# Double-buffering the hidden tile of the scan stage, moving the carry table into its loop, and squaring with an accumulator

## What is computed

```python
x = L0_attn_x
x = x + _L0_attn_ref(_layernorm(x), W, lam_logit, eta, gamma, beta)
#   z = x @ W.T ; m_t = lam[k] * m_(t-1) + z_t  for 4 decays k
#   h = z + sum_k eta[k] * m[..., k] ; layer norm of h, * gamma + beta
x = x + _L0_ffn_ref(_layernorm(x), SU_ug, SU_dp, ...)
#   fwht(x * SU_ug)/64 -> W_up, W_gate -> silu(gate) * up
#   -> fwht(. * SU_dp)/64 -> W_down
```

## Time and profile before

| what | value |
|---|---|
| time, median of 2 runs | 6996.12 us (6816.88 and 7175.36) |
| profiled execution, its own time | 6800.32 us |
| its span on the slowest core (core 7) | 6798.7 us |
| spans of the 8 cores | 6772.5 to 6798.7 us |
| busy: PE, DVE, ACT | 51%, 35%, 14% of the span |
| tables end, first prefix chunk starts | 62.4 us |
| scan stage, its first `pz` to its last store | 1067.3 to 2025.6 us |
| up/gate stage starts | 2463.0 us |

### The profile page before, as it was taken

How to read it: one execution, slowest core, us unless ns; L and a number is a source line. 1 busy time by engine, 2 the same in 40 slices (tenths; PEclk the granted TensorE clock), 3 DMA queues, 4 the chain that set the end, 5 groups by cost and what they waited for, 6 DMA issues and landing times.

```text
span 6798.7 us, 50228 instructions; the slowest of 8 cores (6772.5 to 6798.7 us)
## 1 busy us (share of the span) xinstructions
PE 3484.6 (51%) x16543; PEld 1515.4 (22%) x16543; DVE 2380.4 (35%) x2879; ACT 956.1 (14%) x2027; POOL 220.8 (3%) x423
## 2 busy tenths in 40 slices
PE   0111114222661179999999999211121494756652
PEld 0000001000220024444444444000000142322321
DVE  5565562111446611111111111355434532332322
ACT  3444440000112230000000000211121000000000
POOL 0000001000000000000000000000000110000100
PEclk9999997656765579999999999555555797888876
DMA  4445449999111111111111111211321563645453
GB/s 76 85 84 85 85 69 121 126 124 124 58 68 44 54 33 59 57 56 56 56 56 56 60 60 53 61 50 50 81 68 50 145 181 92 179 107 162 125 155 67
DMA packets 413911, 574.26 MB, mean 84 GB/s; under 512 B 34201, under 2 KB 329693, under 8 KB 403421
## 3 DMA queue, kind: packets, MB, share of 16 engines
q1 hardware_dynamic: 355710, 403.25, 19.3%
q0 software_dynamic: 57952, 167.81, 18.7%
HBM read 638.05 MB, written 167.77 MB: 119 GB/s over the span
## 4 chain that ended last, share of the span: by engine, by line
PE 45%; DVE 24%; DMA 12%; issue 7%; ACT 6%; SPq 4%; another core or an unknown queue 1%; DVEq 1%; ACTq 0%; POOL 0%; POOLq 0%
PE pd L1141 13%; PE pu L912 13%; PE pg L919 13%; DMA x_dram<-hb 5%; DMA ep<-x_dram 4%; DVE statc L413 3%; DVE vq L1009 3%; DVE btmp L1007 3%; PE pz L644 2%; DVE vq L1011 2%; SPq L978 2%; ACT vq L991 1%; PE pq L987 1%; SPq L1026 1%
## 5 line engine op out<-in xcount | busy, mean ns | idle before, releaser
L1141 PE MATMUL pd<-wdsl,v2sl 128*128 128x512 bf16 x4096 | 903.8, 383 | 424.6 <-DMA v2sl<-v_dram 356.3
L912 PE MATMUL pu<-uT_s,wslab 128*128 128x512 bf16 x4096 | 907.0, 380 | 0.8 <-ACT uT_s L861 0.8
L919 PE MATMUL pg<-uT_s,gslab 128*128 128x512 bf16 x4096 | 904.9, 379 | 0.0
L934 DVE SCALAR_TENSOR_TENSOR vtmp<-pu,wsupT,silb 128x1024 f32<-128x1024 f32 x128 | 164.3, 1283 | 1550.9 <-ACT silb L928 1550.9
L987 PE MATMUL pq<-vq,h_s 128*128 128x256 bf16 x512 | 183.1, 372 | 834.4 <-DMA vq<-v_dram 748.8
L1141 PEld LDWEIGHTS pd<-wdsl,v2sl 128*128 128x128 bf16 x4096 | 402.0, 99 | 926.5 <-issue 459.0
L1149 DVE TENSOR_TENSOR acc<-acc,pd 128x512 f32<-128x512 f32 x512 | 351.9, 687 | 636.0 <-PE pd L1141 636.0
L644 PE MATMUL pz<-wzT_s,xlnT_s 128*128 128x512 bf16 x1024 | 296.8, 462 | 515.3 <-DVE carry_bf L696 514.1
L912 PEld LDWEIGHTS pu<-uT_s,wslab 128*128 128x128 bf16 x4096 | 401.3, 98 | 485.8 <-issue 4.1
L919 PEld LDWEIGHTS pg<-uT_s,gslab 128*128 128x128 bf16 x4096 | 400.6, 98 | 483.4
L470 PE MATMUL pp<-w4b,wzT_s 128*128 128x4 bf16 x1792 | 63.4, 166 | 680.2 <-DVE wzT_s L459 680.2
(11 more groups left out here) (146 smaller groups left out, 2140.9 us busy)
## 6 DMA issues: line engine op xcount, KB each, us to landing
v2sl<-v_dram SPq DMA_DIRECT2D x256, 512.0 KB, 10.3
wzT_s<-xfull POOLq DMA_DIRECT2D x112, 512.0 KB, 5.7
G<-xown SPq DMA_DIRECT2D x32, 1024.0 KB, 6.7
wup_bf<-wupT POOLq DMA_DIRECT2D x16, 2048.0 KB, 186.0
wgate_bf<-wgateT POOLq DMA_DIRECT2D x16, 2048.0 KB, 509.5
wslab<-wup_bf SPq DMA_DIRECT2D x512, 64.0 KB, 2.0
gslab<-wgate_bf SPq DMA_DIRECT2D x512, 64.0 KB, 2.0
v_dram<-vchB SPq DMA_DIRECT2D x64, 512.0 KB, 2.8
```

What stands on the lines that cost most here:

```text
L912: last = pe.matmul(pu[par][:, s * 512:(s + 1) * 512], wslab[w % 2][:, c * 256 + jj * 128: c * 256 + (jj + 1) * 128], uT_s[:, c * T + hh * ...
L919: last = pe.matmul(pg[par][:, s * 512:(s + 1) * 512], gslab[w % 2][:, c * 256 + jj * 128: c * 256 + (jj + 1) * 128], uT_s[:, c * T + hh * ...
L934: m_stt_prev = DV.emit(lambda dv, jc=jc, par=par: dv.scalar_tensor_tensor(vtmp2[:, :], pu[par][:, :], wsupT[:, jc:jc + 1], silb2[:, :], AL ...
L1141: last = pe.matmul(pd[par][:, :], v2sl[sp_][:, jj * T + tch * 128: jj * T + (tch + 1) * 128], wdsl[sp_][:, jj * 512:(jj + 1) * 512], start ...
```

## The change

Four edits. The order of the matmuls stays.

- **Two hidden tiles.** `hb` becomes `hb2[0]` and `hb2[1]`. The last addition of the tail writes x2 into `G[b]`, and the store reads `G[b]`. The wait of the copy out of `ph` on the store of j - 1 is gone. In its place SP waits ahead of load(j), and DVE ahead of the last addition, for the store of j - 2 (semaphores `SYX2[b]`). The next stage's loads from `x2_dram` wait for stores 14 and 15.
- **The `am` table.** The 16 rounds of `coef4` ahead of the chunks are gone. Each scan iteration makes its own block in `amc[b]`, at the top of the iteration: two DVE operations, `Exp` on ACT, a third DVE operation.
- **Squares of own chunks.** The two squares are written with `accum_out`, in bfloat16 into a scratch `sqA`, and the two DVE sums L492 and L496 are gone.
- **Memory.** `am` and the top-level `G2h` go; `G2h` is allocated with the buffers of the second norm, where it is also used.

The diff, cut to its core:

```diff
-        for jj in range(TC):
-            coef4(lambda jj=jj: am[:, jj * 128:(jj + 1) * 128], 128.0 * jj + 1.0)
...
-            msq = AC.emit(lambda ac, b=b: ac.activation(G2h[:, :], G[b][:, 0:1024], AF.Square))
-            DV.wait(AC, msq)
-            mr0 = DV.emit(lambda dv: dv.reduce_sum(statc[:, 2:3], G2h[:, :], axis=AX.X))
-            AC.wait(DV, mr0)
-            msq2 = AC.emit(lambda ac, b=b: ac.activation(G2h[:, :], G[b][:, 1024:2048], AF.Square))
+            AC.wait(AC, AC.n)
+            AC.emit(lambda ac, b=b: ac.activation(sqA[:, :], G[b][:, 0:1024], AF.Square,
+                                                  accum_out=statc[:, 2:3]))
+            AC.wait(AC, AC.n)
+            msq2 = AC.emit(lambda ac, b=b: ac.activation(sqA[:, :], G[b][:, 1024:2048], AF.Square,
+                                                         accum_out=statc[:, 6:7]))
             DV.wait(AC, msq2)
-            DV.emit(lambda dv: dv.reduce_sum(statc[:, 6:7], G2h[:, :], axis=AX.X))
-            DV.wait(DV, DV.n)
...
         for j in range(TC):
             b = j % 2
+            if j >= 2:
+                DV.wait(PE, m_hmm_par.get(b, 0))
+            DV.wait(DV, DV.n)
+            DV.emit(lambda dv, j=j: dv.tensor_scalar_add(a4t[:, :], grid4_s[:, :],
+                                                         128.0 * j + 1.0))
+            DV.wait(DV, DV.n)
+            mx_ = DV.emit(lambda dv: dv.tensor_scalar(
+                a4t[:, :], a4t[:, :], scol[0:4, 1:2], None, ALU.mult))
+            AC.wait(DV, mx_)
+            my_ = AC.emit(lambda ac: ac.activation(a4t[:, :], a4t[:, :], AF.Exp))
+            DV.wait(AC, my_)
+            m_amc[b] = DV.emit(lambda dv, b=b: dv.tensor_scalar(
+                amc[b][:, :], a4t[:, :], scol[0:4, 2:3], None, ALU.mult))
...
-                if j >= 1:
-                    DV.wait(SYX2, m_x2st[j - 1])
-                m_hev = DV.emit(lambda dv, hh=hh, par=par: dv.tensor_copy(
-                    hb[:, hh * 1024:(hh + 1) * 1024], ph2[par][:, :]))
+                m_hev = DV.emit(lambda dv, hh=hh, par=par, b=b: dv.tensor_copy(
+                    hb2[b][:, hh * 1024:(hh + 1) * 1024], ph2[par][:, :]))
...
             if j >= 2:
                 SY.wait(DV, m_x2dv[j - 2])
+                SY.wait(SYX2[b], m_x2st[j - 2])
...
+            if j >= 2:
+                DV.wait(SYX2[b], m_x2st[j - 2])
+            mx2 = DV.emit(lambda dv, b=b: dv.tensor_add(G[b][:, :], hb2[b][:, :], G[b][:, :]))
...
-            mst = SYX2.emit(lambda sy, j=j: sy.dma_start(
-                out=x2_dram[j * 128:(j + 1) * 128, :], in_=hb[:, :]))
+            mst = SYX2[b].emit(lambda sy, j=j, b=b: sy.dma_start(
+                out=x2_dram[j * 128:(j + 1) * 128, :], in_=G[b][:, :]))
...
-            SY.wait(SYX2, m_x2st[j])
+            SY.wait(SYX2[b], m_x2st[TC - 2 + b])
```

More of the change, by code:

```diff
@@ L128, in build_nc @@
     SYG = [SubQ(SY), SubQ(SY)]
-    SYX2 = SubQ(SY)
+    SYX2 = [SubQ(SY), SubQ(SY)]
     SYW = [SubQ(SY), SubQ(SY)]
@@ L142, in build_nc @@
     GPX3 = [SubQ(GP) for _ in range(3)]
-    SUBS = [SYG[0], SYG[1], SYX2, SYW[0], SYW[1], SYV[0], SYV[1],
+    SUBS = [SYG[0], SYG[1], SYX2[0], SYX2[1], SYW[0], SYW[1], SYV[0], SYV[1],
             SYVQ[0], SYVQ[1], SYV2[0], SYV2[1],
@@ L175, in build_nc @@
         aloc = sb("aloc", [4, 128], BF16)
-        am = sb("am", [4, TC * 128], BF16)
+        amc = [sb(f"amc{i}", [4, 128], BF16) for i in range(2)]
         a4t = sb("a4t", [4, 128], F32)
@@ L191, in build_nc @@
         G = [sb(f"G{i}", [128, D], F32) for i in range(2)]
-        G2h = sb("G2h", [128, 1024], F32)
         onesb = sb("onesb", [1, 128], BF16)
@@ L372, in build_nc @@
         zbf = stA.enter_context(nc.sbuf_tensor("zbf", [128, D], BF16))
-        hb = stA.enter_context(nc.sbuf_tensor("hb", [128, D], F32))
+        hb2 = [stA.enter_context(nc.sbuf_tensor(f"hb{i}", [128, D], F32)) for i in range(2)]
         Hh = [stA.enter_context(nc.sbuf_tensor(f"H{i}", [128, D], BF16)) for i in range(2)]
+        sqA = stA.enter_context(nc.sbuf_tensor("sqA", [128, 1024], BF16))
         GPB.emit(lambda gp: gp.dma_start(out=gam_b[0:1, :], in_=gammain[:, :]))
@@ L630, in build_nc @@
         first_ph0 = True
+        m_amc = [0, 0]
+        m_hmm_par = {}
         for j in range(TC):
             b = j % 2
+            if j >= 2:
[11 more added lines that the diff above has]
+                amc[b][:, :], a4t[:, :], scol[0:4, 2:3], None, ALU.mult))
             for hh in range(2):
@@ L656, in build_nc @@
                 PE.wait(AC, m_zev[hh])
-                PE.wait(DV, max(m_M, m_ccast, m_phdv[par]))
+                PE.wait(DV, max(m_M, m_ccast, m_phdv[par], m_amc[b]))
                 if first_ph0 and par == 0:
@@ L660, in build_nc, with hmm @@
                     first_ph0 = False
-                def hmm(pe, j=j, hh=hh, par=par):
+                def hmm(pe, j=j, hh=hh, par=par, b=b):
                     last = None
@@ L668, in hmm @@
                         pe.matmul(ph2[par][:, psl], aloc[:, :], carry_bf[0:4, sl], start=False, stop=False)
-                        last = pe.matmul(ph2[par][:, psl], am[:, j * 128:(j + 1) * 128],
+                        last = pe.matmul(ph2[par][:, psl], amc[b][:, :],
                                          marow[0:4, sl], start=False, stop=True)
@@ L714, in build_nc @@
             DV.wait(DV, DV.n)
-            DV.emit(lambda dv, sp=sp: dv.tensor_scalar(
-                hb[:, :], hb[:, :], statc[:, sp + 1:sp + 2], statc[:, sp + 4:sp + 5],
+            DV.emit(lambda dv, sp=sp, b=b: dv.tensor_scalar(
+                hb2[b][:, :], hb2[b][:, :], statc[:, sp + 1:sp + 2], statc[:, sp + 4:sp + 5],
                 ALU.add, ALU.mult))
             DV.wait(DV, DV.n)
-            DV.emit(lambda dv: dv.tensor_mul(hb[:, :], hb[:, :], gam_b[:, :]))
+            DV.emit(lambda dv, b=b: dv.tensor_mul(hb2[b][:, :], hb2[b][:, :], gam_b[:, :]))
             DV.wait(DV, DV.n)
-            mx2 = DV.emit(lambda dv, b=b: dv.tensor_add(hb[:, :], hb[:, :], G[b][:, :]))
+            if j >= 2:
+                DV.wait(SYX2[b], m_x2st[j - 2])
+            mx2 = DV.emit(lambda dv, b=b: dv.tensor_add(G[b][:, :], hb2[b][:, :], G[b][:, :]))
             try:
@@ L741, in build_nc @@
         HhB = [stB1.enter_context(nc.sbuf_tensor(f"HB{i}", [128, D], BF16)) for i in range(2)]
+        G2h = stB1.enter_context(nc.sbuf_tensor("G2h", [128, 1024], F32))
         su_b = stB1.enter_context(nc.sbuf_tensor("su_b", [128, D], F32))
```

3 lines of the change are left out of this document (2 added, 1 removed).

## The result

The changed kernel takes 6868.54 us at the median of 24 runs (6719.9 to 7296.85), the kernel before 6923.61 us at the median of 23 (6793.07 to 7288.82). The ratio is 0.9898, 95% interval 0.9862 to 0.9935. So the gain is 1.0%, between 0.65 and 1.4%.

A forecast was written before the change was run, and what follows sets the result against it. In the stretch it touches, the prediction saw DMA filled by the casts and L676 waiting 354.8 us for the store of `hb`. Terms 23.7 + 38.9 + 0 + 19.1 + 2 = 83.7 us off 6800.3 gave 6716 us, range 6655 to 6800.

The forecast's parts named there:

- Table rounds ahead of the chunks: Start of the kernel: the 16 serial table rounds before the first prefix chunk go, 23.7 us gained, bounds 22 and 24.
- Squares: Own chunks: two squares without the DVE sums save 2.4 us a chunk, 38.9 us for 16, bounds 32 to 42.
- The store wait under the casts: Scan iterations during the weight casts: L676's stall becomes a longer stall for the load of G, period stays 88.6 us, gain nothing.
- The end of the casts: Mixed scan iteration 7: load landed by about 1708.5, only the tail is left, one gain of 19.1 us, bounds 19 and 22.
- After the casts: Last eight scan iterations: 4.4 to 4.9 us replaces 4.86, gain 0.25 us a period, 2 us; bounds 12 lost, 27 gained.
- from the first `ph` matmul to L676 1793.15 - 1791.21 = 1.94: Scan iteration after the casts: last part of the 4.41 us expected between tail and copy out of ph, 1.94 us.
- 4.86 stood: Scan iteration after the casts, kernel before: 4.86 us from the end of L721 to L676, released by the store.
- the table block takes the place of the store: Scan iterations after the casts: the table block fills the removed store wait; without it about 2.9 us less would stand there.
- second rival: After the casts the table round lies fully on the path, costing 12 us, total 6745; sign a period above 37; chance 0.07.
- slower by clock: Up/gate stage: 8192 matmuls lose the higher clock level, 17 us per 1%, 6888 us at 10%; chance 0.03.
- The stall really goes: Scan iterations under the casts: load takes 43.5 us without queueing, period 52.2, gain 184 us there, total 6554; chance 0.08.
- The loop pays for the table: Scan loop: table round fully on the path after the casts, -12 us, only 5 of 19 us come, total 6745; chance 0.07.

The follow-up runs named there:

- the last experiments: Changed kernel with paced casts and the table between the halves, plus the removed store wait put back: 6398.96 and 6398.0 us; without that wait 6321 to 6323, once 6376.

## Why the prediction was right and where it was wrong

- **Table rounds ahead of the chunks, 23.7 us.** Right. The chunk stage starts 22.0 us earlier, 23.7 counted from the first round.
- **Squares, 38.9 us.** Right: 4.95 became 2.49 us a chunk, and the squares alone move the scan stage by 35 to 40 us. With the table it was 61 us to the first x2 store, and the sum had 62.6.
- **The store wait under the casts, 0 us.** Right, and shown from both sides. 354.8 us of waiting for the store became 350.3 us of waiting for the load; putting the wait back leaves the period of 89 us as it is. Changing the load's place in its queue brings 7 us a period, changing its queue 35, and pacing the casts 53.
- **The end of the casts, 19.1 us.** Right: that iteration takes 18.6 us less than before in the mean. (The load of that iteration landed at 1709.72 in the kernel before, 1.2 us later than the 1708.5 that I took from the DMA share.)
- **After the casts, 2 us gained.** Wrong in sign. The step that failed is the term "from the first `ph` matmul to L676 1793.15 - 1791.21 = 1.94", with the "about 0.5 more if PE does these matmuls at its lower level". PE starts the `ph` matmuls 2.25 us behind the tail, near the 2.47 of the sum, but from the first of them to the copy it is 3.15 us and not 1.94. The 1.94 came from the second half of an iteration, where PE had paused for only 1.41 us; here it pauses for 3.7 to 5.4, and the first matmul takes 0.59 us and not 0.38. So the copy starts 5.4 us behind the tail on core 0, in all eight iterations, and not 4.4 to 4.9. The other side of the comparison was off too: "4.86 stood" was one iteration, and the mean of the kernel before is 5.1 on core 7. The statement under the term, that the table block takes the place of the store, is right, and its price is higher than the 2.9 us I gave: 4.0 to 4.6 us a period by the experiments.

  The period grew by 0.3 to 0.9 us on the 8 cores instead of falling by 0.25, about 5 us lost in eight iterations. On cores 0, 1, 6 and 7 it grew by 0.56 us in the mean: 0.33 ahead of the first copy out of `ph` (5.41 and 5.08 us behind the tail), 0.11 between the two copies and 0.11 behind the second. On cores 2 to 5 there are 0.9 us more between the copies, and their up/gate matmuls were slower as well, so I do not put that down to the change. With paced casts all cores have a period of 36.4 to 36.7 us, beside 36.3 before in the mean: a smaller loss, and no gain. The prediction named a period above 37 as the sign of its second rival; cores 2 to 5 show 37.0 to 37.2, the others 36.5 to 36.7.
- **The sum.** 23.7 + 38.9 + 19.1 - 5 = 77 us against 83.7 forecast. The traces have 73.7 by the last x2 store. The ratio says 1.02% of about 6810, 70 us, with an interval from 44 to 94.
- **The range.** The step that failed is the one that says "my number is to be held against executions like that one". The range was laid around one execution of 6800.3 us, though the two runs that I had, 6816.88 and 7175.36 us, have a median of 6996.12. The median of all executions of the changed kernel, 6868.54, lies 149 us above its lowest, and that of the kernel before, 6923.61, lies 131 us above its own. The 3% for "slower by clock" was the only place where the text allowed for it. The range of the gain was right; a range for the median needed this spread in it.
- **Rivals.** "The stall really goes" is out for this change. "The loop pays for the table" named the true direction of the small term: 5 us of the 12 it priced. The up/gate stage takes as long as before: its matmuls have means of 380 and 379 ns before and after on core 0, and 379 or 380 in the profiles of the wait put back, of the table between the halves and of the paced casts, which share the change. On cores 2 to 5 of the one profile of the changed kernel they take 387 to 395.
- **What I did not price.** I priced the edits only as they stand together. Apart, the two hidden tiles give 50 us, of which the table block in the loop takes 33 back; the table costs 24 us ahead of the chunks and 36 in the loop. The prediction has (0.45 + 2.9) x 8 = 27 us as its upper bound, but did not draw the conclusion: keep the second tile and leave the table where it was, or put it between the halves.

## What to carry to other kernels

Before a wait is removed, ask which transfer lands next in the same queue. Here a load stood behind the store, and while the casts ran a second buffer only changed the name of the wait. When they had ended it was worth 4 us an iteration, as long as nothing else was put in the store's place. When a transfer of 1 MB takes 43 us in one stretch and 5 in another, look for the bulk work that shares the DMA engines, and for whether it must be done then: spreading 32 casts over a stage that had room was worth 350 us, about five times what the whole change gave. And put small work that crosses engines where both wait anyway; at the top of a loop it stands ahead of the copies that used to overlap.

## What was not expected of the hardware

- A second hardware queue is served beside the first at the same rate. With the software queue full of casts, one hardware queue moved 1 MB in 43 us; with two of them active each still took 44 to 46 us. I had expected 65.
- A longer pause also slows what comes behind it. With the `Exp` ahead of the copy of `pz`, PE paused 3.7 to 5.4 us ahead of the first `ph` matmuls and ran them at a granted clock of 0.50, 0.59 us for the first one; with 1.4 us of pause the first one took 0.38. That is 1 us of the 4 that the table block costs. The granted clock of a stretch of 160 us was 0.77 without the block there, 0.71 with it, and 0.70 to 0.73 on the 8 cores with it and paced casts. The store wait in the last experiments costs 4.5 us a period without that: it is the distance from 1.4 to 5.7 us between the tail and the copy.
- A cast of 4 MB to 2 MB between DRAM tensors lands in 19 to 20 us when no other cast is under way.
